# Moving the first attention tile's inverse root ahead of the last batch's output scaling, in a one-core perceiver kernel

## The reference, cut to what matters

```python
x = x + cross_attention(ctx_1024, layernorm(x))   # 16 batches, 64 latents, 1601 tokens + 64 latents as keys, 16 heads
x = x + attention(layernorm(x))                   # differential attention, per batch of 64 rows, causal
x = x + experts(layernorm(x))                     # 8 experts, best 2 gated by a softmax

# inside attention(): A1, A2 are two causal softmaxes of each of 16 heads
O = (A1 - lam * A2) @ V
rms = sqrt(mean(O * O, axis=-1) + EPS)            # over the 16 columns of a head
O = O / rms * rms_scale * (1 - LAMBDA_INIT)
return O.reshape(...) @ Wo.T
```

## Time and profile before

| | us |
|---|---|
| median of three runs | 988.33 |
| lowest, highest | 987.59, 992.7 |
| profiled execution, its own time | 989.81 |
| its span in the profile | 988.1 |

### The profile page before, as it was taken

The page is one execution under the profiler, slowest core; times in us unless marked ns, Lnnn a source line. Parts: engine busy times, 40 slices in busy tenths (PEclk is TensorE's granted clock), DMA queues, the critical chain, the costliest instruction groups (busy, mean ns, idle before and its releaser), DMA issues.

```text
span 988.1 us, 20490 instructions
## 1 busy us (share of the span) xinstructions
PE 920.4 (93%) x8246; PEld 494.5 (50%) x8246; DVE 786.7 (80%) x1591; ACT 704.7 (71%) x1003; POOL 377.1 (38%) x376
## 2 busy tenths in 40 slices
PE   7569999999999999999999999999999999979975
PEld 5344445454545454545454545454545454557742
DVE  5968898888787878797979797878786866668965
ACT  4566878787878787878787878787878667535631
POOL 6562034242524242424243425242424132253243
PEclk9799999999999999999999999999999999979987
DMA  6202031303030212120212121212122100000000
GB/s 206 68 17 64 4 88 12 80 12 81 12 79 16 77 17 75 18 74 19 74 19 74 20 72 19 74 24 68 24 56 29 29 1 23 1 23 23 2 6 16
DMA packets 74565, 41.95 MB, mean 42 GB/s; under 512 B 62276, under 2 KB 69864, under 8 KB 74472
## 3 DMA queue, kind: packets, MB, share of 16 engines
q1 hardware_dynamic: 74184, 39.60, 16.9%
q10 hardware_dynamic: 288, 1.05, 0.3%
HBM read 25.98 MB, written 0.59 MB: 27 GB/s over the span
## 4 chain that ended last, share of the span: by engine, by line
PE 66%; DVE 21%; ACT 5%; issue 4%; DMA 1%; POOL 1%; SPq 0%; POOLq 0%; ACTq 0%; DVEq 0%
PE S L2086 8%; PE S L2077 8%; PE S L2080 8%; PE OA L2110 7%; PE OA L2113 7%; PE OA L2116 7%; PE WW L2023 7%; DVE mx L1469 6%; DVE region L1481 4%; DVE region L1460 2%; ACT region L1791 2%; PE WW L2050 1%; PE WW L2051 1%; PE WW L2052 1%; DVE amx L764 1%
## 5 line engine op out<-in xcount | busy, mean ns | idle before, releaser
L1791 ACT ACTIVATE region<-S,sigma 128x1024 f16<-128x1024 f32 x208 | 231.9, 1115 | 155.5 <-PE S L2086 154.4
L1481 DVE TENSOR_TENSOR region<-S,region 128x1024 f16<-128x1024 f32 x208 | 252.5, 1214 | 72.6 <-ACT S L1795 72.6
L1469 DVE TENSOR_REDUCE mx<-WW 128x1 f32<-128x512 f32 (+1 forms) x480 | 259.8, 584 | 34.2 <-PE WW L2023 28.4
L1795 ACT ACTIVATE S<-S,sigma 128x1024 f32<-128x1024 f32 x208 | 225.3, 1083 | 0.0
L2077 PE MATMUL S<-region,xT 128*128 128x512 f16 (+1 forms) x416 | 124.2, 380 | 4.2 <-DVE region L1481 3.3
L2023 PE MATMUL WW<-xT,region 128*128 128x512 f16 x360 | 122.2, 381 | 4.1 <-DVE mx L1469 2.5
L2110 PE MATMUL OA<-region,xk 128*128 128x512 f16 (+1 forms) x416 | 124.2, 380 | 0.0
L2086 PE MATMUL S<-region,xT 128*128 128x512 f16 (+1 forms) x416 | 124.2, 380 | 0.0
L2113 PE MATMUL OA<-region,xk 128*128 128x512 f16 (+1 forms) x416 | 124.1, 380 | 0.0
L2116 PE MATMUL OA<-region,xk 128*128 128x512 f16 (+1 forms) x416 | 123.9, 379 | 0.0
L2080 PE MATMUL S<-region,xT 128*128 128x512 f16 (+1 forms) x416 | 123.7, 379 | 0.0
(11 more groups left out here) (315 smaller groups left out, 1800.6 us busy)
## 6 DMA issues: line engine op xcount, KB each, us to landing
raw<-ctx SPq DMA_DIRECT2D x16, 768.0 KB
rb<-inv_dram SPq DMA_DIRECT2D x16, 512.0 KB, 3.7
xT<-xk SPq DMA_TRANSPOSE x48, 3.3
left_row<-left_pT SPq DMA_DIRECT2D x48, 2.0 KB
raw<-ctx SPq DMA_DIRECT2D x16, 32.5 KB
WO_lo<-L_xattn_Wq ACTq DMA_DIRECT2D x1, 512.0 KB, 3.8
WO_hi<-L_xattn_Wkv ACTq DMA_DIRECT2D x1, 512.0 KB, 4.7
lx<-x SPq DMA_DIRECT2D x1, 512.0 KB, 8.3
```

The source lines that it names most:

```text
L1469: nc.vector.tensor_reduce(mx[:, r, c:c + 1], W[BANK[("m", n)]][:, 0:width], AX.X, ALU.max)\
L1481: nc.vector.tensor_tensor(p_lo[k], src, p_hi[k], ALU.subtract).then_inc(lo_done.sem, 1)
L1791: nc.scalar.activation(p_hi[k], src, ACT.Exp, scale=sigma[:, 0:1])
L1795: nc.scalar.activation(src, src, ACT.Exp, scale=sigma[:, 0:1]).then_inc(e_done.sem, 1)
```

## The change

GpSimd runs inverse_rms(0) ahead of the four multiplications by `rb`. `outputs_low` then follows directly, ahead of inverse_rms(1). ScalarE casts the outputs in step 2, behind `side_copies(1)`, not at the end of step 1. No instruction is added or removed, and no wait.

```diff
             denominators(pool, nc.gpsimd, LAST)
+            inverse_rms(Turn(0))
             normalise_outputs(pool, nc.gpsimd, LAST)
-            for n in range(TB):
+            outputs_low(pool, nc.gpsimd, LAST)
+            for n in range(1, TB):
                 inverse_rms(Turn(n))
-                if n > 0:
-                    ln_deviation(pool, n - 1)
+                ln_deviation(pool, n - 1)
                 if n == X1_SIDE:
                     ln_deviation(pool, TB)
-                if n == 1:
-                    outputs_low(pool, nc.gpsimd, LAST)
             ln_deviation(pool, TB - 1)
...
                 if m > 1:
                     side_copies(m - 1)
+                if m == 2:
+                    for k in range(2):
+                        outputs_high(LAST, k)
...
                 if m + 1 < TB:
                     exp(t.plus(1), 1)
-                if m == 1:
-                    for k in range(2):
-                        outputs_high(LAST, k)
```

## The result

| us | before | after |
|---|---|---|
| median (14 runs each) | 989.88 | 986.21 |
| lowest | 987.59 | 984.13 |
| span of the profiled execution | 988.1 | 984.6 |

The ratio of after to before is 0.9969, with a 95% interval of 0.9956 to 0.9981. One of before's 14 runs took 1202.84 and is not counted in the ratio; without it the median of before is 989.5. So the change is worth 0.3%, some 3 us, and 6.8 were forecast. Sign and place were right, the size was not.

A forecast was written before the change was run, and what follows sets the result against it. TensorE, busy 93% of the span, was taken to bound the kernel, with the change acting on the first tiles behind the loop. With holds the gain summed to 6.8 us: 988.33 - 6.8 = 981.5; 8 of 10 range 978.2 to 986.3.

The forecast's parts named there:

- Root of tile 0: First tiles behind the loop: GpSimd's root runs 868.34 to 871.24, the multiplications by rb starting 0.9 us later than before.
- The collision, first two holds: VectorE's two-SBUF-input instructions stand until GpSimd's running multiplication ends: L802 done at 872.74, L778 held 1.0 us.
- VectorE with holds: Tile 0 on VectorE: L778 held 1.0 us and L790 2.1 by GpSimd, so combine(1) ends at 881.0.
- TensorE, where it counts: Tail on TensorE: full clock, waits of 1 and about 1.2 us, side_transposes(2) at 887.4 instead of 894.22, 6.8 us earlier.
- Casts and low parts, tile 1's root: Casts cost ScalarE nothing; tile 1's root, queued behind outputs_low, runs 882.3 to 885.2, its 1.3 us wait hidden by 0.1.
- No hold: Rival: L802, L778 and L790 aren't held by GpSimd; gain 9.1 us, time 979.2; chance 0.18.
- GpSimd gets in first, or is never left: Rival: L512 beats L787, or L802 is held through all four multiplications; gain 4.5 to 5.2 us; chance 0.24.
- The half clock moves: Rival: TensorE's half clock falls on 886 to 896, where it alone holds the chain; costs up to 5.1 us, 986.6; chance 0.10.
- What would show it: List of trace signs, among them no half clock before 940; wrong if L1133 of tile 1 comes later than 890.

The follow-up runs named there:

- e5: The changed kernel with 14 extra identity products on TensorE in step 2, in its wait for VectorE's first L811; 985.1 us, ratio to before 0.9959.
- e1: The kernel before with only GpSimd's inverse_rms(0) moved ahead of the four multiplications; 984.3 us, ratio to before 0.9941.
- e8: The changed kernel again, unaltered, in another execution; 986.6 us, ratio to before 0.9962.
- e3: The changed kernel with outputs_low put behind inverse_rms(1) and ln_deviation(0); 983.41 us, ratio to before 0.9942.
- e4: The changed kernel with outputs_low on VectorE behind keys(4) in step 2 instead of on GpSimd; 981.92 us, ratio to before 0.9937.
- e7: The changed kernel with outputs_low cut to 4 columns of each half, the rest not computed; 980.68 us, ratio to before 0.9914.
- e2: The kernel before with only ScalarE's two casts moved behind side_copies(1), GpSimd's order unchanged; 988.03 us, ratio to before 0.9987.
- e6: The kernel before with 28 extra identity products on TensorE ahead of side_transposes(1); 988.2 us, ratio to before 0.9986.

## Why the prediction was wrong, step by step

**Root of tile 0: right.** L926 starts at +3.54 (forecast 868.34, +3.55) and takes 2.90.

**The collision, first two holds: right.** L802 of tile 0 at +6.90 with 1.07 (forecast +6.9 and about 1.0), L778 0.93 with its hold (forecast 1.0 of hold; it was 0.76). VectorE also gets in between two GpSimd instructions that stand back to back: L802 ended 0.28 behind the first multiplication (869.91, 870.19), with the second in the queue, and the second took 1.45 instead of 1.28.

**VectorE with holds: the failed step.** "I take a hold to the end of the running instruction" was applied to instructions that read two SBUF tensors. L790's hold came as forecast (2.34 - 0.43 = 1.9, forecast 2.1). But L795, with one SBUF input, stood for the second L512: 1.52 - 0.17 = 1.35, forecast 0. The first L811 came at +17.08, not at +16.2 (881.0), since the other holds were 0.4 shorter than forecast. `keys(4)` and TensorE's `weigh_values(2)` came later with it (+21.87, forecast +20.6). A slip of the sum adds 0.2 here: 881.0 and the 4.47 that the rows give from L811 to the end of keys (885.55 to 890.02) make 885.5, not 885.3. The Trainium skill, "SBUF — State Buffer", which the prediction cites, says in its section "Who interferes with whom" that `tensor_scalar` can, where its operands meet the conditions, enter a two-port mode and so stand against GpSimd, and that `tensor_reduce` on this chip never does. The traces agree on both sides: L795 and L646 (`tensor_scalar`) were held, 1.52 and 2.16, L792 (`tensor_reduce`), which ran beside the second L512, not, 0.42. In which mode L795 ran, no view shows. The prediction named the two-port mode and priced only the two-input half.

**TensorE, where it counts: the second failed step, and the larger.** The prediction let the stretch run "at full clock". From the two traces of the changed kernel and that of e5: +28.23 forecast; 29.48 at full clock (e5), so 1.25 for L795's hold (1.35) and the small terms beside it; 31.34 and 32.73 at half clock, so 1.9 and 3.3 for the dip. 28.23 + 1.25 + 1.86 = 31.34. The gain at the second L811 was 3.7 instead of 6.8. The forecast of 6.8 had thus counted the end of the old dip, about 1.8 us by the estimate above, as a gain, for no other reason than that the new waits would be about 1 us. With a dip in both kernels, or (by that estimate) in neither, the gain is 3.7. From there to the last L811 but two it was carried along, as forecast (41.1 in both, 41.1 to 41.2 in e1 to e8).

**Casts and low parts, tile 1's root: right.** The casts cost ScalarE nothing (`queries(4)` follows them at once, at 875.79). L926 of tile 1 starts at +17.25 (forecast 882.3, +17.5), and its wait behind `outputs_low` is hidden by keys(4), with 1.4 to spare (it ended at 882.37, keys(4) at 883.83). The forecast had 0.1 to spare; most of the difference is L795's hold, which made keys(4) late.

**The rivals.** "No hold" is out by four held instructions. "GpSimd gets in first, or is never left" is out too: L787 started at 874.58 and L512 at 874.96, and L802 came after one multiplication. "The half clock moves" is the one that came in part, at a chance of 0.10. Its price was put at up to 5.1. Found were 1.9 and 3.3 against the full clock of e5; in e8 the stretch at the lower level was as long as before (10.2 us by the granted clock), but its start lay on products behind which TensorE waits for keys(4) in any case (0.70 in e5). That its 986.6 lies near the measured 986.21 is luck: it took off too much for the clock and nothing for L795, and it stands on a median of before of 988.33, which was 989.5 in the comparison. Its chance was too low. The argument against it was that the old wait was 4.17 long and the new ones about 1. L795's hold made the new wait 2.28 (about 0.9 without it, an estimate: 2.28 - 1.35). In e1 it was 2.14, for ScalarE's copy behind the casts. Both came with the half clock; e3, e4 and e7, whose longest waits there were under 1, had none.

**The signs.** Two of those under "What would show it" came: a half clock before 940, and L1133 (now L1132) of tile 1 later than 890, that is +25.2. It started at +25.43.

## What to carry to other kernels

An early start on GpSimd can be paid for by VectorE where the two overlap on SBUF: go through VectorE's instructions in that overlap one by one, `tensor_scalar` and two-input ones alike, and put GpSimd's long ones beside VectorE work that reads PSUM. When a long wait of TensorE is shortened to some 2 us, ask whether its clock falls with the shorter wait too. A forecast that lets the new stretch run at full clock, where the old one had a dip, counts the end of the dip as a gain and has to say why it should end. And where a step of 4 us on GpSimd holds VectorE for most of that time, VectorE may as well do it (2.35 against 4.40 here, in the complete version with the lowest median).

## What the runs showed of the hardware that was not expected

A VectorE instruction of 16 columns took 1.52 us instead of 0.17 beside a GpSimd subtraction, and one of 128 columns 2.16 instead of 0.34. GpSimd's pair of subtractions in its turn grew from 4.21 to 4.40 where a VectorE instruction got in between. Not every overlap holds, though. Beside GpSimd's powers L926 (2.9 us) and L641 (0.54) VectorE's instructions of the same two kinds kept their usual length in these traces: L637, a `tensor_scalar` of one column, took 0.15 inside L926, and a later L802 took 0.43 inside L641 (after the change, GpSimd first, then VectorE):

```profile
937.72 0.54 POOL L641 TENSOR_TENSOR ln<-ln,mhalf 128x1 f32<-128x1 f32 x1
```

```profile
937.84 0.43 DVE L802 TENSOR_TENSOR Oc<-Ob,oms 128x256 f32<-128x256 f32 x1 [0.70 <-DVE lg L843]
```

No run here shows why these differ from the subtractions and multiplications.

TensorE's clock fell to its lower level with waits of 4.54 (e2), 4.17 (before), 2.28 and 2.29 (the change, twice), 2.14 (e1) and 1.81 us (e6), in e1, e2, e6 and before while TensorE still waited, in the changed kernel 1 to 2 us after it had gone on. With 14 products in the place of the 2.28 (3.29 us of work) it stayed up.
